# A sequence-mixing kernel's lead reordered: first grams, key spreads, loads and weight pieces

## The chip, the cores and the metric

The kernel runs on one core of one Trainium2 chip. The metric is the time of one execution on the device in microseconds. The four compute engines are TensorE (PE), VectorE (DVE), ScalarE (ACT) and GpSimd (POOL); SyncE (SP) issues all transfers. Each engine takes its own instructions in order and waits on semaphores.

## The reference

Four layers follow each other on a hidden state of 4 sequences x 1024 tokens x 128 channels, each ending in a layer norm over its residual sum:

```
x = layernorm(x + delta_attention(x))   # q, k, v: projection, causal conv of 4 taps, silu
x = layernorm(x + moe(x))               # 8 experts, top 2, 128 -> 256 -> 128, gelu
x = layernorm(x + lru(x))               # gated linear recurrence over tokens
x = layernorm(x + ffn(x))               # gated 128 -> 512, two 512 x 512 gelu layers, 512 -> 128
```

The delta attention has 4 heads of 32 and chunks of 32 tokens. q and k are normalised; per chunk the product of keys with keys (the gram), scaled by beta, is a strictly lower triangular 32x32 matrix A, and T = inverse of (I + A) is needed before the chunk's state step. The state runs through the chunks in order:

```
attn = tril(q_i @ k_i.T);  u_new = u_i - w_i @ S     # u = T v beta, w = T k beta
o_i  = q_i @ S + attn @ u_new;  S = S + k_i.T @ u_new
```

## The kernel before

Tokens are cut into 8 tiles of 128 tokens of all 4 sequences (512 columns, 16 chunks). Most operands are held as two parts (high and low) so that one product is three matmuls. The convolution is folded into the projection: `project(t, m)` is 12 matmuls of 512 columns (4 taps x 3), for m = k, q, v.

For each tile the attention front is: `beta`, `project`, `heads_in` (ACT: silu and square), `squares` (PE: sums per head), `norms_ln` and `norms_exp` (ACT), `unit_rows` (DVE: normalised keys and queries, and turned keys), `key_spread(t, g)` (ACT: keys laid out by head, two halves of 8 chunks), `gram(t, g)` (PE, two halves), `gram_rows(t, g)` (DVE). For every pair of tiles `solve_in` (DVE) turns the grams so that POOL can solve all 128 triangles at once, in 31 rows of two operations (`solve`); `solve_out` (DVE) turns the result back and scales it. The rows are then stored (`store_pack`, `store_tt`) and come back tile by tile. The delta chain of a tile has four steps of `delta_wu` (PE), `delta_spread` (DVE), `delta_attn` (PE), `delta_qp` (DVE), `delta_state` (PE), `delta_out` (DVE); the spread of T by heads is `t_spread` on POOL.

The order of the work is written out by hand, one list for each engine. The lead does the front of tiles 0 to 4 (`LEAD = 5`, lines 368, 499, 860 and 1382). `ramp1(0, 5)` runs the delta chain of tile 0 beside the front of tile 5, `ramp2(0, 6)` the end of tile 0's attention beside the front of tile 6, `dense(0, 1)` the experts of tile 0 (loop over e = 0 to 7) beside the delta chain of tile 1, `ramp3(0, 1, 7)` the recurrence of tile 0, the attention end of tile 1 and the front of tile 7. From then on `dense` and `tails` alternate; the steady ones are not touched.

Weights come from memory in 19 pieces of 512 columns through two buffers (piece p uses buffer p mod 2); `split_pieces` on DVE cuts each into parts. Pieces 0 to 3 and 8 are also centred (four operations more, piece 8 one more for its scaling). In which stage a piece is split is in the table `PIECES`, by stage number. Piece p is loaded (`load_piece`) once piece p - 2 has been split. Buffer 1 lies over the scratch tile m4 of the recurrence. The raw tile `xs` has one buffer: `load_xs(t)` waits for `beta(t-1)` and `split_x(t-1)`, and `split_x(t)` on DVE cuts it into one of two slots. SP's lists are at lines 363 to 403: in the lead, each turn issues `load_xs(t + 2)`, then pieces, then `store_pack(t)`.

In the lead PE does for each tile: squares of t, beta and all three projections of t + 1, then gram(t). DVE ends the lead with `solve_out(0)`; the first `solve` on POOL (line 1148) stands before `ramp1`, whose `t_spread(0, 0)` needs `solve_out(0)`. `ramp1` on PE starts with `project(5, 0)` and `beta(5)`.

## Time and profile before

| | |
|---|---|
| median of 3 runs | 907.69 us (902.43 to 908.14) |
| the profiled execution, its span | 902.85 us, 900.7 us |
| TensorE busy | 815.4 us, 91% of the span |
| VectorE, ScalarE, GpSimd busy | 618.7, 490.2, 480.7 us (69, 54, 53%) |
| mean granted TensorE clock | 0.949 of full speed |
| chain that ended last | PE 57%, DVE 15%, POOL 10%, issue 10%, ACT 5%, DMA 2% |

The rows of a timeline are: start us, length us, engine, line and operation, tile written <- tiles read, shape, count, and in brackets how long the engine had been idle before and what ended that. Line 429 is the helper through which every matmul goes and line 1340 the second half of splitting a piece, so the tile names tell the work. A matmul row's length runs over the start of the next, since matmuls are pipelined. The busy share of PE is not PE at its peak. The lead lasts to about 105 us, ramp1 to 141, ramp2 to 170, dense(0) to 222, ramp3 to 265.

### The profile page before, as it was taken

To read this page: it belongs to the slowest core of one execution; us is meant where nothing else is said; L and a number is where in the kernel's file an instruction comes from. 1 tells how busy PE (TensorE), PEld (TensorE's weight loads), DVE (VectorE), ACT (ScalarE), POOL (GpSimd) and SP (SyncE) were. 2 spreads that over 40 slices of the span, in tenths; PEclk is the share of its full clock that TensorE was granted. 3 is DMA by queue.
4 is the path that set the end of the run, shared out by engine and by line. 5 is a ranking of instruction groups with operands and counts; after the bars stand their busy time and mean duration, and the time that the engine had idled before them with its cause. 6 is when DMAs were issued, how large, how long until landed. Compare 5 with 4: busy or idle time off the path is not lost.

```text
span 900.7 us, 11912 instructions
## 1 busy us (share of the span) xinstructions
PE 815.4 (91%) x3810; PEld 628.3 (70%) x3810; DVE 618.7 (69%) x1166; ACT 490.2 (54%) x768; POOL 480.7 (53%) x508
## 2 busy tenths in 40 slices
PE   5998798897778999999998999999999999999896
PEld 3786685676457777777776778768867886676674
DVE  2777776787759758676867677767677766676352
ACT  2887145334653474357435744575476447667553
POOL 0049697676716637863785355534544453366343
PEclk9999699599969999899999999999999999999998
DMA  3134606301220020002000300200020000000000
GB/s 128 48 99 113 187 1 176 118 12 30 53 59 25 24 59 1 1 25 70 1 1 10 109 1 1 70 24 0 0 70 24 0 0 12 1 0 13 1 12 12
DMA packets 37759, 35.81 MB, mean 40 GB/s; under 512 B 1616, under 2 KB 30544, under 8 KB 37712
## 3 DMA queue, kind: packets, MB, share of 16 engines
q1 hardware_dynamic: 37712, 35.22, 14.0%
q8 instruction: 25, 0.41, 0.2%
q14 instruction: 22, 0.18, 0.1%
HBM read 21.85 MB, written 13.37 MB: 39 GB/s over the span
## 4 chain that ended last, share of the span: by engine, by line
PE 57%; DVE 15%; POOL 10%; issue 10%; ACT 5%; DMA 2%; POOLq 0%; DVEq 0%; ACTq 0%; SPq 0%
PE bank L429 57%; POOL tpm L1133 2%; POOL tmp L1130 2%; POOL fbl L1189 2%; DVE sexp L1428 2%; POOL acc L1197 2%; DVE spread L1412 1%; DVE yg L1438 1%; DMA ws<-in_wf 1%; DVE m L1473 1%; POOL fbl L1220 1%; ACT L1084 1%; POOL fal L1228 1%; DVE fbh L1605 1%; DVE fah L1662 1%
## 5 line engine op out<-in xcount | busy, mean ns | idle before, releaser
L1001 ACT ACTIVATE hf<-bank 128x512 f32<-128x512 f32 x64 | 38.3, 598 | 182.5 <-PE bank L429 176.0
L1189 POOL TENSOR_TENSOR fbl<-hf,fbh 128x512 fp32r<-128x512 f32 x64 | 81.9, 1279 | 81.9 <-DVE fbh L1605 81.9
L1130 POOL TENSOR_TENSOR tmp<-apm,tpm 128x31 f32<-128x31 f32 (+15 forms) x124 | 77.2, 622 | 54.4 <-DVE apm L1302 47.1
L1220 POOL TENSOR_TENSOR fbl<-hf,fbh 128x512 fp32r<-128x512 f32 x32 | 41.3, 1290 | 103.3 <-DVE fbh L1662 103.3
L429 PEld LDWEIGHTS bank<-pk,spread 128*128 128x128 f32 x640 | 82.7, 206 | 18.7 <-DVE spread L1412 11.7
L429 PE MATMUL bank<-pk,spread 128*128 128x64 f32 x640 | 85.2, 291 | 7.4 <-DVE spread L1412 5.6
L1603 DVE TENSOR_TENSOR fbl<-hf,fbh 128x512 fp32r<-128x512 f32 x64 | 59.2, 925 | 34.2 <-ACT fbh L1007 31.7
L1197 POOL TENSOR_TENSOR acc<-acc,yg 128x512 f32<-128x512 f32 x48 | 64.3, 1340 | 33.6 <-DVE yg L1438 33.6
L1133 POOL TENSOR_TENSOR tpm<-tpm,tmp 128x31 f32<-128x31 f32 (+15 forms) x124 | 76.8, 620 | 9.7
L429 PE MATMUL bank<-fal,wfh 128*128 128x512 f32 x160 | 68.3, 427 | 2.7 <-ACT hf L1033 1.6
L1216 POOL TENSOR_TENSOR fal<-hf,fah 128x512 fp32r<-128x512 f32 x32 | 41.6, 1301 | 51.8 <-DVE fah L1657 51.8
L1438 DVE TENSOR_TENSOR yg<-bank,gb 128x512 f32<-128x512 f32 x64 | 43.8, 685 | 35.4 <-PE bank L429 35.3
L429 PE MATMUL bank<-fbl,wmh 128*128 128x512 f32 x128 | 58.8, 460 | 8.4 <-POOL fbl L1189 4.9
L1033 ACT ACTIVATE hf<-bank,vec 128x512 f32<-128x512 f32 x64 | 42.5, 686 | 42.4 <-PE bank L429 42.1
L1228 POOL TENSOR_TENSOR fal<-hf,fah 128x512 fp32r<-128x512 f32 x32 | 41.4, 1298 | 40.6 <-DVE fah L1662 40.6
L429 PE MATMUL bank<-fah,wfh 128*128 128x512 f32 x160 | 62.5, 391 | 0.0
L429 PE MATMUL bank<-fah,wfl 128*128 128x512 f32 x160 | 62.5, 390 | 0.0
L429 PE MATMUL bank<-fbl,wfh 128*128 128x512 f32 x128 | 55.1, 431 | 7.6 <-POOL fbl L1220 7.5
L429 PE MATMUL bank<-x1l,wmh 128*128 128x512 f32 x128 | 55.5, 434 | 0.0
L429 PE MATMUL bank<-x1h,wmh 128*128 128x512 f32 x128 | 52.2, 408 | 0.0
L429 PE MATMUL bank<-x1h,wml 128*128 128x512 f32 x128 | 51.8, 405 | 0.0
L429 PE MATMUL bank<-fbh,wfh 128*128 128x512 f32 x128 | 51.4, 401 | 0.0
(220 smaller groups left out, 2234.9 us busy)
## 6 DMA issues: line engine op xcount, KB each, us to landing
pk<-pack SPq DMA_DIRECT2D x7, 1280.0 KB, 7.1
pack<-pk SPq DMA_DIRECT2D x5, 1280.0 KB, 6.7
ws<-in_wf SPq DMA_DIRECT2D x11, 256.0 KB, 3.5
pack<-pk SPq DMA_DIRECT2D x4, 640.0 KB, 4.4
xs<-in_xh SPq DMA_DIRECT2D x8, 262.0 KB, 4.3
xt<-in_xh SPq DMA_DIRECT2D x8, 262.0 KB, 3.0
ws<-in_wm SPq DMA_DIRECT2D x8, 256.0 KB, 2.7
tt<-ttp SPq DMA_DIRECT2D x4, 512.0 KB, 3.0
```

The lines of the kernel that those rows point to most:

```text
L429: return P.matmul(out, lhsT, rhs, start=start, stop=stop, skip_group_check=skip)
L1001: A.activation(hf[:, 0, :], bank[4][:, :], ACT.Gelu).then_inc(S["gelu_done"], 1)
L1033: A.activation(hf[:, o % 2, :], bank[4 + o][:, :], ACT.Gelu, scale=vec[:, v + o:v + o + 1])\
L1130: G.tensor_tensor(m, a, r, ALU.mult).then_inc(S["t_mul"], 1)
L1133: G.tensor_tensor(o, o, m, ALU.subtract).then_inc(S["t_step"], 1)
L1189: G.tensor_tensor(fbl[:, sl, :], hf[:, 1, :], f32(fbh[:, sh, :]), ALU.subtract)\
L1197: G.tensor_tensor(acc[:, :], (x1 if e == 1 else acc)[:, :], yg[:, (e - 1) % 2, :], ALU.add)\
L1216: G.tensor_tensor(fal[:, c, :], hf[:, c % 2, :], f32(fah[:, c, :]), ALU.subtract)\
L1220: G.tensor_tensor(fbl[:, o, :], hf[:, o % 2, :], f32(fbh[:, o, :]), ALU.subtract)\
L1228: G.tensor_tensor(fal[:, o, :], hf[:, o % 2, :], f32(fah[:, o, :]), ALU.subtract)\
L1438: tt(yg[:, e % 2, :], bank[6][:, :], gb[:, e % 2, :], ALU.mult).then_inc(S["yg_ready"], 1)
L1603: tt(fbl[:, sl, :], hf[:, 0, :], f32(fbh[:, sh, :]), ALU.subtract).then_inc(S["lo0"], 1)
```

## The change

- Lead, PE: after squares(0), beta(1) and projections (1, k) and (1, q) come squares(1), gram(0), beta(2), gram(1), and only then projection (1, v) and those of tile 2. From tile 2 on the order is as before, but the last turn (tile 4) also does beta(5) and projections (5, k) and (5, q) ahead of gram(4).
- The second half of the key spread of tiles 0 and 1 is one DVE operation (`first_spread`, 128x1024) instead of four ACT copies.
- Lead, DVE: solve_in(0) follows gram_rows(1), ahead of the pieces 0 and 1 and value_rows(1). solve_out(0) moves ahead of gram_rows(4), and split_x(6) into the lead.
- SP: load_xs runs further ahead; from the second round on each round is store_pack(t), two pieces, load_xs(t + 3).
- Pieces: `PIECES` is a table by name. Six pieces are split in the lead instead of twelve, two in ramp1 instead of one, two in ramp2 instead of three, six in dense(0) instead of three, three in ramp3 instead of none.
- solve_out(1) and store_tt(1) move from ramp2 into dense(0), split_x(7) from the end of ramp2 into dense(0). The third solve starts in dense(0) (twelve rows there) instead of ramp2 (ten rows there, seven in dense(0)); nineteen rows instead of fourteen are left for ramp3.
- ramp1, PE: starts with projection (5, v); squares(5), projection (6, k) and gram(5) fill the steps. mix_gate stands behind the last step. ACT: beta_in(5) first, heads_in(5, v) last.

```diff
-PIECES = ((0, 1), (2, 3), (4, 5), (6, 7, 8), (9, 10, 11), (12,), (13, 14, 15), (16, 17, 18))
+PIECES = dict(tile1=(0, 1), tile2=(2, 3), tile3=(4, 5), ramp1=(6, 7), ramp2=(8, 9), experts0=(10, 11, 12, 13, 14, 15),
+              ramp3=(16, 17, 18))
 # SP, lead
+            load_pieces(PIECES["tile1"])
             load_x(0)
             load_xs(1)
+            load_xs(2)
+            load_xs(3)
+            store_pack(1)
+            load_pieces(PIECES["tile2"])
+            load_xs(4)
+            store_pack(2)
+            load_pieces(PIECES["tile3"])
+            load_xs(5)
+            store_pack(3)
+            load_pieces(PIECES["ramp1"])
+            load_xs(6)
+            store_pack(4)
             store_tt(0)
 # PE, lead
+            squares(0)
+            beta(1)
+            project(1, 0)
+            project(1, 1)
+            squares(1)
+            gram(0, 0)
+            gram(0, 1)
+            beta(2)
+            gram(1, 0)
+            gram(1, 1)
+            project(1, 2)
+            for m in range(3):
+                project(2, m)
+            for t in range(2, LEAD):
                 squares(t)
+                beta(t + 1)
+                project(t + 1, 0)
+                project(t + 1, 1)
                 if t + 1 < LEAD:
+                    project(t + 1, 2)
                 gram(t, 0)
                 gram(t, 1)
 # DVE, lead
+            def first_spread(t):
+                dve.wait_ge(S["kq_done"], 2 * t + 2)
+                tt(kspread[slot(t)][1], rep(pks[t][:, 8:16, SK:SK + 1, :], 2, NH), heads(8), ALU.mult)\
+                    .then_inc(S["kexp_dve"], 1)
...
+            unit_rows(0)
+            first_spread(0)
+            beta_rows(0)
+            value_rows(0)
+            split_x(2)
+            beta_rows(1)
+            gram_rows(0, 0)
+            gram_rows(0, 1)
+            unit_rows(1)
+            first_spread(1)
+            gram_rows(1, 0)
+            gram_rows(1, 1)
+            solve_in(0)
+            split_pieces(PIECES["tile1"])
+            value_rows(1)
+            split_x(3)
+            for t in range(2, LEAD):
                 unit_rows(t)
                 if t == LEAD - 1:
-                    split_pieces(PIECES[t - 1][2:])
                     solve_in(1)
                 value_rows(t)
+                split_x(t + 2)
                 beta_rows(t)
+                if t == LEAD - 1:
+                    solve_out(0)
+                else:
+                    split_pieces(PIECES[f"tile{t}"])
                 gram_rows(t, 0)
                 gram_rows(t, 1)
 # DVE, dense (m = 0)
-                    if isinstance(m, int) and m == 0 and e in (2, 4, 6):
-                        split_pieces(PIECES[NT - 1][e // 2 - 1:e // 2])
+                    if isinstance(m, int) and m == 0 and e == 1:
+                        solve_out(1)
+                    if isinstance(m, int) and m == 0 and e == 3:
+                        split_x(NT - 1)
+                    if isinstance(m, int) and m == 0 and 2 <= e:
+                        split_pieces(PIECES["experts0"][e - 2:e - 1])
 # DVE, ramps
             def ramp1(a, s):
                 delta_spread(a, 0)
-                split_pieces(PIECES[s])
+                beta_rows(s)
                 delta_qp(a, 0)
                 delta_out(a, 0)
                 delta_spread(a, 1)
+                split_pieces(PIECES["ramp1"][:1])
+                unit_rows(s)
                 delta_qp(a, 1)
-                split_x(s + 1)
...
             def ramp2(a, s):
                 solve_in(2)
-                split_pieces(PIECES[s][:2])
+                split_pieces(PIECES["ramp2"])
                 head_scale(a)
                 unit_rows(s)
                 beta_rows(s)
-                solve_out(1)
...
-                split_pieces(PIECES[s][2:])
-                split_x(s + 1)
             def ramp3(m, a, s):
                 head_scale(a)
                 scale("2", m, m1, m3, x2).then_inc(S["x2"], 1)
+                split_pieces(PIECES["ramp3"][:2])
                 softplus_log()
+                split_pieces(PIECES["ramp3"][2:])
                 lru_input(m)
 # PE, ramp1
-                project(s, 0)
-                beta(s)
+                project(s, 2)
+                pe.wait_ge(S["qkv_act"], 3 * LEAD + 2)
                 delta_wu(a, 0)
-                project(s, 1)
+                squares(s)
                 delta_attn(a, 0)
                 delta_state(a, 0)
                 delta_wu(a, 1)
-                project(s, 2)
+                project(s + 1, 0)
                 delta_attn(a, 1)
                 delta_state(a, 1)
                 delta_wu(a, 2)
-                squares(s)
+                gram(s, 0)
                 delta_attn(a, 2)
                 delta_state(a, 2)
                 delta_wu(a, 3)
-                gram(s, 0)
-                mix_gate(a)
+                gram(s, 1)
                 delta_attn(a, 3)
                 delta_state(a, 3)
-                gram(s, 1)
-                project(s + 1, 0)
+                pe.wait_ge(S["qkv_act"], 3 * LEAD + 3)
+                mix_gate(a)
                 beta(s + 1)
                 project(s + 1, 1)
 # ACT, recurrence of tile 0
+                    act.wait_ge(S["ws_lo"], PIECES["ramp3"][1] + 1)
 # POOL, dense (m = 0)
-                    if isinstance(m, int) and m == 0 and e < E - 1:
-                        solve(2, range(10 + e, 11 + e))
+                    if isinstance(m, int) and m == 0 and e == 1:
+                        solve_init(2)
+                    if isinstance(m, int) and m == 0 and 0 < e < E - 1:
+                        solve(2, range(2 * e - 2, 2 * e))
```

## Rows read from the trace of the kernel before

**Rows 1.** Windows: busy us (instructions) of each engine, granted clock, DMA share, GB/s.
```profile
80.00:100.00 20.00, 16.01 (x74) 13.38 (x73) 17.70 (x28) 8.79 (x16) 17.61 (x29) 0.74 0.42 114
100.00:120.00 20.00, 14.51 (x71) 12.11 (x71) 9.81 (x15) 2.60 (x5) 13.20 (x24) 0.83 0.42 124
```
**Rows 2.** Timeline of PE in the lead and at the start of ramp1.
```profile
24.00 1.98 PE L429 MATMUL bank<-hf,cst 128*128 128x512 f32 x4 [0.38 <-DVE s3row L1379]
...
26.28 0.80 PE L429 MATMUL bank<-xtl,wtaph 128*128 128x512 f32 x1
...
35.17 1.89 PE L429 MATMUL bank<-pk,gb 128*128 128x64 f32 x16
...
88.48 3.38 PE L429 MATMUL bank<-pk,gb 128*128 128x64 f32 x16 [3.87 <-DVE pk L1264]
...
106.58 1.97 PE L429 MATMUL bank<-pk,texp 128*128 128x64 f32 x8 [5.38 <-POOL texp L1159]
```
**Rows 3.** Timeline of POOL: the first solve row, and the spread after it.
```profile
56.41 0.24 POOL L1130 TENSOR_TENSOR tmp<-apm,tpm 128x31 f32<-128x31 f32 x1 [47.06 <-DVE apm L1302]
...
105.28 2.47 POOL L1159 TENSOR_TENSOR texp<-ttp,cst 128x512 f32<-128x512 f32 x2 [5.48 <-DVE ttp L1313]
```
**Rows 4.** Timeline of DVE in the lead.
```profile
62.40 0.43 DVE L1253 CAST xth<-xs 128x524 fp32r<-128x524 f32 x1 [3.23 <-DMA xs<-in_xh]
...
76.62 0.48 DVE L1253 CAST xth<-xs 128x524 fp32r<-128x524 f32 x1 [2.06 <-DMA xs<-in_xh]
...
78.88 0.87 DVE L1338 CAST wmh<-ws 128x512 fp32r<-128x512 f32 x1
...
82.59 0.41 DVE L1291 TENSOR_TENSOR pk<-bank,cst 128x256 f32<-128x256 f32 x1
...
88.22 1.10 DVE L1332 TENSOR_TENSOR ws<-ws,s3row 128x512 f32<-128x512 f32 x1
...
92.71 1.94 DVE L1302 STREAM_TRANSPOSE apm<-kkp 128x1024 f32<-128x1024 f32 x1
...
101.98 1.90 DVE L1311 STREAM_TRANSPOSE ttp<-tpm 128x1024 f32<-128x1024 f32 x1
```
**Rows 5.** Timeline of DVE in ramp1 and ramp2.
```profile
135.66 1.29 DVE L1428 STREAM_TRANSPOSE sexp<-bank 32x128 f32<-32x128 f32 x4 [0.53 <-PE bank L429]
...
149.01 0.43 DVE L1338 CAST wfh<-ws 128x512 fp32r<-128x512 f32 x1 [5.94 <-DMA ws<-in_wf]
...
151.25 0.75 DVE L1455 SCALAR_TENSOR_TENSOR a<-a,vec,a 128x512 f32<-128x512 f32 x1
...
158.18 0.68 DVE L1406 TENSOR_TENSOR x<-bank,a 128x512 f32<-128x512 f32 x1
```
**Rows 6.** Timeline of PE in ramp2 and at the start of dense(0).
```profile
152.05 1.13 PE L429 MATMUL bank<-xt,centre_w 128*128 128x512 f32 x2 [2.66 <-DVE a L1455]
...
173.76 3.68 PE L429 MATMUL bank<-pk,spread 128*128 128x64 f32 x16 [0.90 <-DVE spread L1412]
```
**Rows 7.** Timeline of ACT: the first half of the key spread of tile 0.
```profile
28.38 1.71 ACT L855 ACTIVATE gb<-pk,cst 128x256 f32<-128x256 f32 x4 [0.24 <-DVE pk L1264]
```
**Rows 8.** Timeline of SP, its transfers' issues: a pack store and the next tile's load.
```profile
54.40 0.40 SPq L347 DMA_DIRECT2D pack<-pk  x1
...
56.19 1.07 SPq L326 DMA_DIRECT2D xs<-in_xh  x1
```
**Rows 9.** The page's transfers: KB each, median us from issue to landing.
```profile
xs<-in_xh SPq DMA_DIRECT2D x8, 262.0 KB, 4.3
```
**Rows 10.** Timeline of DVE in dense(0) (two rows) and ramp3 (two rows).
```profile
179.98 0.69 DVE L1603 TENSOR_TENSOR fbl<-hf,fbh 128x512 fp32r<-128x512 f32 x1 [2.37 <-ACT fbh L1007]
...
204.09 0.79 DVE L1603 TENSOR_TENSOR fbl<-hf,fbh 128x512 fp32r<-128x512 f32 x1 [1.12 <-ACT fbh L1007]
...
238.05 0.72 DVE L1463 TENSOR_SCALAR m<-m 128x512 f32<-128x512 f32 x1 [0.71 <-ACT m L918]
...
240.07 0.69 DVE L1406 TENSOR_TENSOR x<-bank,a 128x512 f32<-128x512 f32 x1 [1.30 <-ACT a L883]
```

More of the change, by code:

```diff
@@ L859, in _ @@
             act.wait_ge(S["w_in"], 32)
-            for t in range(LEAD):
+            for m in range(3):
+                heads_in(0, m)
+            beta_in(0)
+            A.preload_act_table_set(LN_EXP)
+            norms_ln(0)
+            norms_exp(0)
+            act.wait_ge(S["sp_step"], 1)
+            A.activation(spv[:, 1:2], spv[:, 0:1], ACT.Exp, scale=-1.0).then_inc(S["sp_step"], 1)
+            A.preload_act_table_set(SILU)
+            heads_in(1, 0)
+            key_spread(0, 0)
+            heads_in(1, 1)
+            beta_in(1)
+            A.preload_act_table_set(LN_EXP)
+            norms_ln(1)
+            norms_exp(1)
+            key_spread(1, 0)
+            A.preload_act_table_set(SILU)
+            heads_in(1, 2)
+            for t in range(2, LEAD):
                 for m in range(3):
@@ L1180, in ramp3 @@
                 t_spread(a + 1, 1)
-                solve(2, range(17, C - 1))
+                solve(2, range(12, C - 1))
             def dense(m, a, f, inv=0):
```

81 lines of the change are left out of this document (30 added, 51 removed).

## The prediction

> **What bounds the kernel now.** I read the windows of the first 120 us first: in 80 to 120 us, where the lead gives way to the first ramp, TensorE has gaps and its granted clock falls to 0.74 and 0.83 of 2.4 GHz [rows 1]. Nothing behind the third ramp is changed, so only the time up to there can move.
>
> The PE timeline names the two gaps [rows 2]. The gram of tile 4 stands 3.87 us behind that tile's normalised keys, since no lead product is left to fill; and the first delta product, at 106.58, stands 5.38 us behind a spread on POOL. After a gap products run at half speed: a gram half that took 1.89 at 35.17 takes 3.38 at 88.48. POOL's first triangular solve starts at 56.41, once the grams of tiles 0 and 1 are through DVE, and ends 5.48 us before 105.28, at 99.80: 43.4 us [rows 3]. DVE turns the result at 101.98 and hands it on 3.2 us later [rows 4]. So the delta chain waits for solve, DVE and POOL in series.
>
> From there to the dense stage DVE sets the end: it stands 5.94 us before a weight piece until 149.01, comes to head_scale at 151.25 [rows 5], and PE waits 2.66 us for it [rows 6].
>
> **The change part by part.**
>
> *Lead: PE and solve.* The squares of tile 0 start at 24.0 as before. From 26.7 to 35.17 run three projections, 2.83 us each; squares take 1.8, a beta 0.86, a gram half 1.75 (1.89 less its drain) [rows 2]. After beta(1) and two projections PE is at 32.4; squares(1) waits for the second activation of tile 1, which stands on ACT behind a table load, an activation pair and key_spread(0,0), four copies in 1.71 us [rows 7]: about 34.8. Both halves of gram(0) end at 38.4, beta(2) at 39.3. DVE takes gram_rows(0) ahead of unit_rows(1), so tile 1's keys come at 40.0, ACT's copies end at 41.75 and gram(1,0) starts at 41.9: a new PE gap of 2.6 us. DVE's key spread (1024 columns) has no row; its bounds are nothing, where it lies wholly beside ACT's copies, and 1.9, as the 1024-column transpose at 101.98 [rows 4]; I take 1.2, and hide it behind those copies and the first gram half, which together last 3.4. gram(1) ends at 45.4, solve_in(0) at 48.3; POOL starts 8 us earlier and ends at 91.7.
>
> PE is then 3.4 us behind the old order with the same work done, so the squares of tile 4 end at 87.8. But the old gap of 3.87 now holds two projections of tile 5.
>
> *Lead: DVE and loads. Here I think the gain is lost.* solve_out(0) stands on DVE behind split_x(6) and beta_rows(4), and split_x(6) needs load_xs(6). SP now goes pack store, two pieces, load_xs, each round. In the old order pack(1) is issued at 54.40, xs(4) at 56.19, and DVE waits 3.23 us for it until 62.40 [rows 4, 8]: 8.0 us from the issue of the store, where the median of such loads is 4.3 [rows 9]. So a load waits for the 1.28 MB ahead of it. The two pieces (0.51 MB) between them add from nothing to 2.7 us (in proportion to 1.54 MB in 8.0 us); I take 1.5, near the middle, so 9.5. Then, with a centred piece at 4.5 less 1.1 for its scaling, 3.35 (88.22 to 92.71), a plain one at 1.86 (two in 78.88 to 82.59), split_x with beta_rows at 2.3 (76.62 to 78.88) and gram_rows at 1.4:
> store_pack(1) needs value_rows(1), behind two centred pieces: 48.3 + 6.7 + 0.7 = 55.7; xs(4) lands at 65.2. store_pack(2) at 65.2 + 2.3 + 6.7 + 1.4 = 75.6; xs(5) at 85.1. store_pack(3) at 85.1 + 2.3 + 3.7 + 1.4 = 92.5; xs(6) at 102.0. Then 2.3, solve_out 3.2, the spread 1.3 and 0.3 of handing on: the first delta product at 109.1, not 106.58: **+2.5**. With the pieces at nothing it is -2, with 2.7 each it is +6. PE has ended project(5,2) near 102 and idles seven us, so half speed follows as before.
>
> The Trainium skill (DMA: Bandwidth & Descriptors, Queues, rings and completion order) says that a completion's semaphore write lands only after every earlier write of that DMA engine; by that rule a load can't be seen before the store ahead of it, and the term would lie above, not below, +2.5.
>
> *Ramp 1.* Before, 29.1 us run from the first delta product to the end of the last state product at 135.66 [rows 2, 5]. Each step is a chain: spread, attention, qp, state, transposes. Step 0 exchanges a projection for the shorter squares (-0.9); step 1 gets piece 6 and unit_rows ahead of qp on DVE (+2.3 beyond its old filler); steps 2 and 3 lose split_x and unit_rows (-1.1). Sum **+0.3**. PE's two projections fewer give nothing: the chain bounds.
>
> *Ramp 2.* DVE's 5.94 wait and two pieces in 2.24, together 8.2, give way to value_rows 0.7, piece 8 with its scaling 4.5 and piece 9 1.86: **-1.1**. PE now waits over 4 us for head_scale, as long as the gap ahead of 88.48, so I charge half speed for its next two products and the variance: **+0.9**. solve_out(1), which leaves its place ahead of the normalisation at 158.18, lay beside ACT's chain; its exposure is between 0 and 3.2, I take **-0.7**, the time of one ACT operation. The piece and split_x that leave the end of the ramp put DVE ahead of the first expert spread, but PE waited only 0.90 for that [rows 6]: **-0.9**. Together with the lead, the dense stage starts at +1.0.
>
> *Dense(0).* DVE gets solve_out(1) at e=1, split_x at e=3 and pieces at e=3, 5, 7, beside those that stood at e=2, 4, 6. A plain piece takes 1.12 alone (149.01 to 151.25) and 1.86 beside POOL, which works here. The idle that stood at these places [rows 10] is 2.37 at e=1, and 1.12 at e=5, and the same once more at e=7. Exposed: 3.2 - 2.4 = 0.8 at e=1, 1.3 + 1.9 at e=3, 0.7 at e=5 and 0.7 at e=7: **+5.4**. POOL gets twelve short rows and two memsets for seven long rows; I charge nothing, covered by its waits for DVE; that cover is the third rival's point.
>
> *Ramp 3.* Three pieces stand around the softplus steps, two before POOL is busy: 1.12 + 1.12 + 1.86 = 4.1, less the idle of 0.71 and 1.30 behind them [rows 10]: **+2.1**. ACT's decay now waits for piece 17 as well, which is done before softplus is. POOL's five more rows, seven us, end in its idle before the next stage.
>
> Sum +1.0 + 5.4 + 2.1 = **+8.5 us**. The profiled execution took 902.85 (span 900.7), 4.8 under the median of 907.69; four executions lie two at 902.4 to 902.9 and two at 907.7 to 908.1. Against the profile the sum is 911.4, against the median 916.2; not knowing the level of the next runs I count from the middle, 905.3: 913.8.
>
> **The rivals.** *The loads are not held* (16%). xs lands 4.3 us after its issue, DVE never waits, solve_out(0) ends at 99.2, the first delta product is at 100.5: -6.1; with -1.0 for full clock in step 0 and +0.3 - 1.1 + 0.9 - 0.7 - 0.9 as above the dense stage starts at -8.6; +5.4 + 2.1 leave -1.1: 904.2. For it: the median of 4.3. Against: 62.40.
>
> *All of it arrives* (16%). As above, and the added DVE work falls into DVE's idle of dense(0) and ramp 3, while the pack store freed from pieces ahead of it gives up to 2.4 more at the start of dense(0): -11, 894.3. Against: the idle stands at other places than the additions.
>
> *DVE and POOL collide in dense(0)* (25%). The place is e=1 to 7, with twelve solve rows on POOL and six pieces on DVE. A piece cost 1.86 instead of 1.12 where they met. If it costs 2.4, and POOL's doubled rows use up the idle of e=5 and 7, the stage pays 0.8 + 3.7 + 2.4 + 2.4 = 9.3 and ramp 3 3 x 2.4 - 2.0 = 5.2: +15.5 with the start's 1.0, 920.8. It decides from pieces over 2.0 us on average. The Trainium skill (SBUF — State Buffer, Who interferes with whom) speaks for this one: a VectorE operation with two SBUF inputs and a reading GpSimd operation exclude each other for whole instructions. By that rule, the trace agrees as far as the 1.86 goes.
>
> **How the numbers follow.** Forecast 43% (from -1 to +13 by its bounds, 904 to 918), rivals 16, 16 and 25. One per cent, 9.1 us, is what a measurement can tell. Slower by more: the third rival's 25 and 9 of the forecast's, 0.34. Faster by more: 0.16. The rest, 0.50. The range, 897 to 922, leaves out most of the second rival and the end of the third.
>
> **What would show it.** DVE's xs casts of tiles 5 and 6 near 85 and 102 behind a DMA (without a wait: first rival); POOL's first solve row near 48; a PE gap of 2.6 near 39; the first delta product near 109; DVE idle gone at e=3 of dense(0) and pieces there over 2.0 (third rival); ramp 3 two us longer. The forecast is wrong if the first delta product comes before 104, or if dense(0) takes no longer than before.

## The result, and the profile of the changed kernel

The changed kernel takes 917.05 us in the median of four runs (914.88 to 918.04), the kernel before 906.03 beside it (902.43 to 908.14): a ratio of 1.0123, 95% interval 1.0081 to 1.0165. It is slower. The middle of the interval lies a little beyond the one per cent that I called the limit of a measurement, and its lower end lies within it. The profiled execution took 914.88 us with a span of 912.9, against 902.85 and 900.7: 12.2 us more in the span, where I had summed 8.5.

The ledger of the two profiled executions, by landmarks that both have. The last columns are for the experiments below.

| landmark (start, us) | before | changed | xs first | piece later | lead | best | relief |
|---|---|---|---|---|---|---|---|
| first delta product | 106.58 | 111.11 | 103.80 | 110.79 | 102.85 | 102.72 | 104.19 |
| last state transposes of ramp1 | 135.66 | 145.40 | 138.89 | 134.13 | 126.69 | 126.15 | 128.00 |
| head_scale of ramp2 | 151.25 | 157.21 | 150.84 | 147.96 | 140.40 | 135.26 | 137.03 |
| attention norm of ramp2 | 158.18 | 163.56 | 157.18 | 155.82 | 148.51 | 144.64 | 146.41 |
| first attention product of dense(0) | 173.76 | 177.00 | 171.18 | 170.18 | 162.71 | 160.95 | 162.37 |
| sum at the end of dense(0) | 221.35 | 227.98 | 222.18 | 221.74 | 215.80 | 211.48 | 210.82 |
| attention norm of ramp3 | 240.07 | 250.31 | 244.51 | 243.89 | 238.10 | 230.38 | 229.66 |
| first spread of dense(1) | 265.95 | 277.88 | 272.08 | 271.82 | 266.01 | 258.72 | 258.61 |
| span | 900.7 | 912.9 | 907.2 | 907.5 | 901.6 | 894.2 | 897.8 |

Between the first two columns: +4.5 at the first delta product, +5.2 in ramp1, -6.5 from there to the dense stage, +3.4 in dense(0), +5.3 in ramp3, and 0.3 in all that follows. Predicted were +2.5, +0.3, -1.8, +5.4 and +2.1.

The last row of the table needs care. Behind the first spread of dense(1) the orders of all kernels here are the same, but eleven of the fourteen profiled executions take 634.8 to 636.0 us from there to the end, and three take 638.8 to 639.5: the projection as filler, the early softplus and relief. So some 4 us of a span can come from a part that no edit touches, and versions are best compared by the rows above.

The windows of the changed kernel, with busy us and instructions of each engine, granted clock, DMA share and GB/s. The first two answer to [rows 1]:

```profile
80.00:100.00 20.00, 20.00 (x113) 16.34 (x111) 11.68 (x20) 15.86 (x29) 11.28 (x22) 1.00 0.62 169
100.00:120.00 20.00, 14.81 (x73) 12.10 (x73) 12.04 (x22) 6.53 (x10) 10.27 (x20) 0.74 0.44 135
120.00:140.00 20.00, 18.25 (x99) 18.01 (x98) 11.26 (x23) 5.18 (x10) 18.16 (x26) 0.63 0.05 13
```

The last window in the kernel before:

```profile
120.00:140.00 20.00, 18.91 (x136) 16.31 (x135) 17.20 (x36) 11.02 (x18) 18.20 (x26) 1.00 0.00 1
```

In 80 to 100 us the change has done what its order says: TensorE has no gap and the upper level of its clock (1.00, against 0.74). But in 120 to 140 us, where the kernel before ran at 1.00, the granted clock is 0.63. The lower level is where ramp1 loses its time.

TensorE's timeline, beside [rows 2] and [rows 6]:

```profile
41.30 1.97 PE L433 MATMUL bank<-pk,spread 128*128 128x64 f32 x16 [2.31 <-issue]
...
105.85 0.77 PE L433 MATMUL bank<-xtl,wtaph 128*128 128x512 f32 x1 [5.18 <-ACT yg L855]
...
111.11 1.25 PE L433 MATMUL bank<-pk,texp 128*128 128x64 f32 x8
...
124.03 1.10 PE L433 MATMUL bank<-qpc,sexp 128*128 128x64 f32 x8 [1.75 <-DVE qpc L1479]
...
126.38 3.62 PE L433 MATMUL bank<-pk,gb 128*128 128x64 f32 x16
...
158.01 1.13 PE L433 MATMUL bank<-xt,centre_w 128*128 128x512 f32 x2 [0.70 <-DVE a L1514]
...
199.02 2.47 PE L433 MATMUL bank<-pk,spread 128*128 128x64 f32 x16 [3.18 <-DVE spread L1471]
```

POOL's, beside [rows 3], and its sum of experts in dense(0):

```profile
49.38 0.24 POOL L1171 TENSOR_TENSOR tmp<-apm,tpm 128x31 f32<-128x31 f32 x1 [39.96 <-DVE apm L1343]
...
108.52 2.50 POOL L1200 TENSOR_TENSOR texp<-ttp,cst 128x512 f32<-128x512 f32 x2 [15.59 <-DVE ttp L1354]
...
191.66 1.75 POOL L1236 TENSOR_TENSOR acc<-acc,yg 128x512 f32<-128x512 f32 x1
```

ScalarE's, the last beta of the lead:

```profile
105.11 0.60 ACT L855 ACTIVATE yg<-bank 128x512 f32<-128x512 f32 x1 [6.04 <-DVE yg L1319]
```

DVE's in the lead, beside [rows 4]:

```profile
88.21 0.43 DVE L1294 CAST xth<-xs 128x524 fp32r<-128x524 f32 x1 [6.38 <-DMA xs<-in_xh]
...
103.23 0.43 DVE L1294 CAST xth<-xs 128x524 fp32r<-128x524 f32 x1 [5.03 <-DMA xs<-in_xh]
...
104.32 0.70 DVE L1319 STREAM_TRANSPOSE yg<-yg 128x512 f32<-128x512 f32 x1
...
105.14 1.98 DVE L1352 STREAM_TRANSPOSE ttp<-tpm 128x1024 f32<-128x1024 f32 x1
```

SP's issues, beside [rows 8]:

```profile
79.18 0.39 SPq L350 DMA_DIRECT2D pack<-pk  x1
79.63 3.16 SPq L336 DMA_DIRECT2D ws<-in_wm  x2
82.89 1.24 SPq L329 DMA_DIRECT2D xs<-in_xh  x1
93.98 0.40 SPq L350 DMA_DIRECT2D pack<-pk  x1
...
97.59 1.22 SPq L329 DMA_DIRECT2D xs<-in_xh  x1
```

DVE's in the ramps and in dense(0), beside [rows 5] and [rows 10]:

```profile
120.14 0.89 DVE L1381 TENSOR_TENSOR wml<-ws,wmh 128x512 fp32r<-128x512 f32 x1
...
123.71 0.27 DVE L1479 TENSOR_TENSOR qpc<-cst,bank 128x128 f32<-128x128 f32 x1
...
152.75 0.65 DVE L1373 TENSOR_TENSOR ws<-ws,s3row 128x512 f32<-128x512 f32 x1
...
157.21 0.74 DVE L1514 SCALAR_TENSOR_TENSOR a<-a,vec,a 128x512 f32<-128x512 f32 x1
...
186.50 1.64 DVE L1381 TENSOR_TENSOR wfl<-ws,wfh 128x512 fp32r<-128x512 f32 x1
...
190.60 1.66 DVE L1296 TENSOR_TENSOR xtl<-xs,xth 128x524 fp32r<-128x524 f32 x1
192.19 1.51 DVE L1379 CAST wfh<-ws 128x512 fp32r<-128x512 f32 x1
...
237.71 1.66 DVE L1381 TENSOR_TENSOR wfl<-ws,wfh 128x512 fp32r<-128x512 f32 x1
...
246.93 0.55 DVE L1379 CAST wfh<-ws 128x512 fp32r<-128x512 f32 x1
...
250.31 0.68 DVE L1465 TENSOR_TENSOR x<-bank,a 128x512 f32<-128x512 f32 x1
```

The first two rows are the last operation of piece 6 and the last of the qpc pair in step 1 of ramp1. Between them stands unit_rows, and it is 3.8 us from the start of the one to the end of the other; TensorE waits 1.75 us of that. From 152.75 to 157.21 are both pieces of ramp2, at 190.60 and 192.19 the split and a piece of expert 3, and at 237.71 and 246.93 pieces of ramp3.

POOL's first solve row comes 7.0 us sooner and the solve ends 15.6 us before POOL's next work, but nothing is gained: its result is turned at 105.14 only, behind split_x(6), which waited 5.03 us for its load. That is the read of the whole lead: what is ready at 92.9 stands in a queue behind something that isn't.

### The profile page after: what moved, and what is told of

Its sections match the earlier page's. It is cut to its first block, busy times and chain, and to the rows that moved or that the text cites. A ratio compares the mean times of both kernels' runs of the same rounds, so it can differ in the third digit from the quotient of the medians.

```text
span 912.9 us, 11905 instructions
## 1 busy us (share of the span) xinstructions
PE 826.6 (91%) x3810; PEld 637.9 (70%) x3810; DVE 623.9 (68%) x1168; ACT 485.6 (53%) x759; POOL 481.6 (53%) x508
## 4 chain that ended last, share of the span: by engine, by line
PE 60%; DVE 19%; ACT 7%; issue 6%; POOL 6%; DMA 1%; SPq 0%; DVEq 0%; POOLq 0%; ACTq 0%
PE bank L433 60%; DVE sexp L1487 2%; DVE yg L1497 1%; DVE spread L1471 1%; DVE m L1532 1%; POOL fbl L1228 1%; POOL acc L1236 1%; DVE fbl L1665 1%; POOL tpm L1174 1%; POOL fbl L1261 1%; POOL tmp L1171 1%; DVE fbh L1667 1%; ACT L1125 1%; DVE x L1465 1%; POOL fal L1269 1%
## 5 line engine op out<-in xcount | busy, mean ns | idle before, releaser
L433 PEld LDWEIGHTS bank<-pk,spread 128*128 128x128 f32 x640 | 84.7, 211 | 21.9 <-DVE spread L1471 11.1
L433 PE MATMUL bank<-pk,spread 128*128 128x64 f32 x640 | 87.4, 296 | 11.5 <-DVE spread L1471 6.8
L433 PE MATMUL bank<-fbh,wml 128*128 128x512 f32 x128 | 51.9, 406 | 0.0
L433 PE MATMUL bank<-fbh,wmh 128*128 128x512 f32 x128 | 51.8, 405 | 0.0
```

The lines of the kernel that those rows point to most:

```text
L433: return P.matmul(out, lhsT, rhs, start=start, stop=stop, skip_group_check=skip)
```

## Experiments

Each is the changed kernel with the edit shown. The kernel before ran beside them, with medians from 903.8 to 904.7.

### The loads ahead of the stores

```
-            store_pack(2)
-            load_pieces(PIECES["tile3"])
             load_xs(5)
-            store_pack(3)
-            load_pieces(PIECES["ramp1"])
+            store_pack(2)
+            load_pieces(PIECES["tile3"])
             load_xs(6)
+            store_pack(3)
+            load_pieces(PIECES["ramp1"])
             store_pack(4)
```

> The changed kernel, with SP issuing load_xs(5) and load_xs(6) ahead of the pack store and the two pieces of their round, nothing else moved. Theory (a load waits behind the store and the pieces issued before it): DVE's casts of xs for tiles 5 and 6, which stood at 88.2 behind 6.4 us and at 103.2 behind 5.0 us of waiting, come near 82 and 98 with almost no wait; with them ACT's activation of beta of tile 5 and PE's last v projection, which waited 5.2 us, move from 105.9 to about 100; the first delta product comes near 104 to 105 instead of 111.1. The whole is 5 to 8 us faster than the changed kernel. Rival (the loads are late by themselves, or DVE is busy anyway): the casts stay within 1.5 us of 88 and 103, and the whole within 2 us.

It took 908.98 us (ratio to before 1.0031, interval 1.0002 to 1.0060). The casts of tiles 5 and 6 start at 81.69 and 96.88 and wait for nothing; project(5, 2) starts at 100.89 and the first delta product at 103.80, 7.3 us sooner than with the change. But ramp1 then takes 35.1 us, and this is its window:

```profile
120.00:140.00 20.00, 20.00 (x91) 19.42 (x91) 8.29 (x20) 0.00 (x0) 17.96 (x28) 0.50 0.05 14
```

Twenty us at the lower level throughout. Of the head start of 7.3 us, 5.7 reach the end of the span, and the loss in ramp1 is a separate one.

### A projection as filler in step 2 of ramp1

```
                 delta_wu(a, 2)
+                project(s + 1, 1)
                 gram(s, 0)
...
                 beta(s + 1)
-                project(s + 1, 1)
```

> The changed kernel with the k-side projection's neighbour, projection (6, q), moved on PE from the end of ramp1 into step 2, ahead of the first gram half of tile 5. No work is added. Theory (in ramp1 the clock fell to half from 125 to 149 us and the steps of 64-column products kept it there, while 512-column projections held it in the kernel before): with a projection in step 2 the clock is back at full speed by step 3, step 3 takes about 7 us instead of 10.5, and ramp1's end comes 2 to 5 us earlier. Rival (the delta chain through DVE bounds each step, the clock only fills idle time): the projection lengthens step 2 by its 2.9 to 5 us and the end comes no earlier, or up to 3 us later.

913.16 us (1.0082, 1.0048 to 1.0116). The gap ahead of step 1's product from qpc is there as before (1.72 us at 122.73), the two products behind it run at the lower level, and then the projection brings the upper level back: the window 120 to 140 has 0.83, and the last step takes 6.0 us instead of 10.2. Step 2 pays for the projection (10.4), so the last transposes come at 141.16, 4.2 us sooner, of which 1.0 was there already at the first delta product (110.11).

### Piece 6 one step later

```
                 delta_spread(a, 1)
-                split_pieces(PIECES["ramp1"][:1])
                 unit_rows(s)
                 delta_qp(a, 1)
                 delta_out(a, 1)
                 delta_spread(a, 2)
+                split_pieces(PIECES["ramp1"][:1])
                 delta_qp(a, 2)
```

> The changed kernel with the split of piece 6 on DVE moved from step 1 of ramp1 (ahead of unit_rows of tile 5) to step 2. Theory (the PE gap of 1.75 us at 122.3 us, made by piece 6 and unit_rows ahead of qp1, is what drops the clock): the gap shrinks to under 0.5 us, the clock stays at full speed in step 2, and the last transposes of ramp1 come 4 to 6 us earlier than 145.4. Rival (the low column count of the steps themselves drops it, gap or not): the clock falls within a few us all the same, and only the 1.4 us of the piece are gained.

910.45 us (1.0066, 1.0033 to 1.0100). The window:

```profile
120.00:140.00 20.00, 18.75 (x137) 16.53 (x137) 16.54 (x37) 8.21 (x17) 18.22 (x25) 1.00 0.10 27
```

The products of steps 1 and 2 on TensorE's timeline:

```profile
121.55 1.09 PE L433 MATMUL bank<-qpc,sexp 128*128 128x64 f32 x8
...
123.36 1.95 PE L433 MATMUL bank<-pk,gb 128*128 128x64 f32 x16
...
125.47 2.00 PE L433 MATMUL bank<-pk,spread 128*128 128x64 f32 x16 [0.16 <-DVE spread L1471]
```

There is no wait before the product from qpc at 121.55, where the changed kernel has 1.75 us, and the gram half behind it takes 1.95 us at the upper level. From the first delta product to the last transposes the ramp takes 23.3 us against 34.3: 1.5 us of DVE's work at the wrong place cost 11. By steps, 1.9 of the 11 are step 1, with the wait in it, and 8.8 are steps 2 and 3 at the lower level (10.0 and 10.2 us against 5.7 and 5.7). The steps' products are the same in both runs, so their small size alone didn't lower the clock: the rival falls. This is the largest single thing that the runs found. Of the 11.3 us won there, 6.8 are left at the first attention product of dense(0): now DVE's chain of solve_in(2) and both pieces is what head_scale waits for, beside POOL's second solve, which had ended before in the slow ramp.

### The third solve and solve_out(1) back in ramp2

```
-                solve(2, range(12, C - 1))      # POOL, ramp3
+                solve(2, range(17, C - 1))
...
+                solve_init(2)                   # POOL, ramp2
+                solve(2, range(10))
...
                 beta_rows(s)                    # DVE, ramp2
+                solve_out(1)
                 attention_norm(a)
```

In dense(0) one row stands at each of experts 0 to 6 again, and solve_out(1) leaves expert 1.

> The changed kernel with one part undone: solve_out(1) is back in ramp2, and POOL's third solve starts in ramp2 with ten rows, seven in dense(0) and fourteen in ramp3, as before the change. Pieces and split_x stay where the change put them. Theory (what dense(0) and ramp3 cost is DVE's own queue of pieces): dense(0) gets shorter by 1 us or less, ramp3 by at most 1, the whole is within 2 us. Rival (POOL's doubled rows beside DVE's pieces make the cost, by collisions): dense(0) gets shorter by 3 us or more and ramp3 by 2, the whole is 4 us faster.

915.27 us (1.0126, 1.0079 to 1.0173): no gain in total. Dense(0) is not shorter (51.9 us from its first attention product, against 51.0), so neither the short rows nor solve_out(1) were what lengthened it. But ramp3, from the sum to the first spread, takes 46.1 us instead of 49.9; the kernel before took 44.6. Nine profiled executions with nineteen rows left for ramp3 and no edit in it take 49.8 to 50.4 us there, so five solve rows more or less on POOL are 3.8 of ramp3's 5.3 us. What is gained so is paid before it: the dense stage starts 1.9 us later, with solve_out(1) in ramp2, and takes 0.9 more.

### The lead: three edits together

The loads first, `beta_rows(4)` ahead of `split_x(6)` on DVE, and piece 6 one step later.

> Three edits to the lead and first ramp together: the xs loads of tiles 5 and 6 are issued ahead of the pack stores, the last lead tile's beta rows stand ahead of the split of tile 6 on DVE, and piece 6 stands in step 2 of the first ramp. Theory (the lead's two waits and one late DVE wait that costs TensorE its clock): the first delta product comes near 103.8, the ramp runs at the upper level in 23.5 us, its last state transposes stand near 127.5 against 145.40 with the change, the dense stage starts 12 or more us earlier, and of that 9 to 12 us reach the end: 903 to 906. Rival (what is won ahead of the ramp is given back to the loads of the second ramp, which wait for its first pack store): the end comes at 909 to 912 as with each edit alone.

902.02 us, ratio to before 0.9968 (0.9945 to 0.9990): a little better than I expected, and faster than both kernels (than the kernel before by 0.3 per cent). The two losses add up: the first delta product at 102.85, ramp1 in 23.8 us, the dense stage 14.3 us sooner than with the change. By the first spread of dense(1) 11.9 of them are left; 2.1 were lost in dense(0), 0.3 in ramp3.

### Beta rows alone

```
-                split_x(t + 2)
-                beta_rows(t)
+                if t == LEAD - 1:
+                    beta_rows(t)
+                split_x(t + 2)
+                if t < LEAD - 1:
+                    beta_rows(t)
```

> The changed kernel with one edit: in the last lead round beta_rows(4) stands on DVE ahead of split_x(6), which waits 5.03 us for its load, instead of behind it. Theory (the missed step: beta_in(5) on ACT waits for these rows, and project(5,2) for beta_in(5)): project(5,2) starts near 92 to 98 instead of at 105.85, and is done before the solve is turned; but the first delta product still waits for solve_out(0), behind the same load, so it comes at 109.5 to 110.5 instead of 111.11, and the total stays within 2 us of 917. Rival (the projection at half speed is what holds the first delta product): it comes at 107 or earlier, and the total falls by 4.

918.34 us (1.0165, 1.0122 to 1.0208). Project(5, 2) starts at 100.45, later than I expected but done before the turn, and the first delta product comes at 108.94, 2.2 us sooner, but now behind a gap, and at the lower level. TensorE's timeline:

```profile
108.94 1.94 PE L433 MATMUL bank<-pk,texp 128*128 128x64 f32 x8 [5.42 <-issue]
110.68 3.73 PE L433 MATMUL bank<-hf,cst 128*128 128x512 f32 x4
```

Four square products take 3.73 us instead of 1.94, and the last transposes come at 146.30. What the late projection had cost it had given back as a warm clock: alone, the edit is worth nothing.

### Ramp2: head_scale ahead of the pieces

```
                 solve_in(2)
-                split_pieces(PIECES["ramp2"])
                 head_scale(a)
                 unit_rows(s)
                 beta_rows(s)
+                split_pieces(PIECES["ramp2"])
                 attention_norm(a)
```

> As the kernel with three edits to the lead and first ramp, and in the second ramp pieces 8 and 9 stand on DVE behind head_scale, unit_rows and beta_rows instead of ahead of them. Theory (head_scale stands behind 6 us of pieces, and TensorE waits 3.8 us for it and falls to half speed): head_scale comes 5 to 6 us sooner, TensorE's gap ahead of the product from a shrinks below 1 us, the products of the gram and the router in this ramp run at the upper level, and the dense stage starts 4 to 6 us sooner than without this edit. Rival (the ramp is bound by DVE's total work): the pieces are then late for the attention norm and the start of the dense stage moves by under 2 us.

It has the three edits of the lead too: 901.56 us (0.9963, 0.9945 to 0.9982). head_scale comes at 135.54, 4.9 us sooner, and the norm at 148.09, 0.4 us sooner. DVE waits 3.36 us for a transfer ahead of unit_rows and then does both pieces while ScalarE's 1 / deviation has been ready since 143.6. The dense stage starts at 162.27 instead of 162.71. The rival was right: the pieces were late for the norm instead.

### Dense(0): the split of tile 7 at expert 6

```
-                    if isinstance(m, int) and m == 0 and e == 3:
+                    if isinstance(m, int) and m == 0 and e == 6:
                         split_x(NT - 1)
```

> The changed kernel with one edit: the split of tile 7's input stands at expert 6 of dense(0) on DVE instead of expert 3. Theory (the 2.1 us of split ahead of fbl, the transposes and the spread of expert 3 are what TensorE waits for): its wait of 3.18 us for the third delta spread of dense(0) falls to about 1.1, and dense(0) takes 1.5 to 2.5 us less than its 50.98, the total 915. Rival (DVE's total work bounds dense(0)): the wait turns up at expert 6 and 7, dense(0) takes what it took, 917.

918.37 us (1.0147, 1.0105 to 1.0190). TensorE's wait for the third spread falls from 3.18 to 1.89, and another of 2.86 appears ahead of the down product at 224.09 (it was 1.37); dense(0) takes 52.1 us. The rival held: moving work within the stage moves the wait.

### Dense(0): six subtractions made twice

```
+                    if p in PIECES["experts0"]:
+                        tt(low_of(p), buf_of(p)[:, :], f32(high_of(p)), ALU.subtract).then_inc(S["sub_once"], 1)
+                        dve.wait_ge(S["sub_once"], p - PIECES["experts0"][0] + 1)
                     tt(low_of(p), buf_of(p)[:, :], f32(high_of(p)), ALU.subtract).then_inc(S["ws_lo"], 1)
```

> The changed kernel with the subtraction of pieces 10 to 15 made twice, the second behind the first; what is computed is the same. Six more two-input operations of DVE in dense(0), 0.93 to 1.65 us each by the trace, 8 to 9 us of DVE's time. Theory (DVE's queue bounds dense(0), and each us of piece there is a us of the stage but for the two idle places behind the spreads): dense(0) grows from 50.98 by 5 to 8 us, so the price of a piece there is about 70 to 100 per cent of its time, and the six pieces and one split explain the whole difference to the kernel before. Rival (TensorE's own work and gates bound it, and pieces fall into the wait for yg): it grows by under 3 us.

920.97 us (1.0188, 1.0149 to 1.0228). The second subtractions take 0.69, 0.75, 0.79, 0.86, 0.97 and 0.96 us, 5.0 together where I had expected 8 to 9, and dense(0) takes 56.6 us instead of 51.0, 5.6 more: each us of DVE's time at the places of the pieces is a us of the stage, with nothing hidden. At expert 1 it isn't so: with solve_out(1), 3.2 us, taken out there (and POOL's rows put back) the stage took 51.9. TensorE's waits in the stage:

```profile
186.72 2.00 PE L433 MATMUL bank<-pk,spread 128*128 128x64 f32 x16 [0.64 <-DVE spread L1474]
...
201.17 3.67 PE L433 MATMUL bank<-pk,spread 128*128 128x64 f32 x16 [4.62 <-DVE spread L1474]
...
217.78 2.13 PE L433 MATMUL bank<-pk,spread 128*128 128x64 f32 x16 [2.07 <-DVE spread L1474]
```

The wait for the third spread grows from 3.18 to 4.62 and for the fourth from 1.24 to 2.07.

### The softplus steps in the lead

```
             value_rows(1)
             split_x(3)
+            softplus_log()
...
                 split_pieces(PIECES["ramp3"][:2])
-                softplus_log()
                 split_pieces(PIECES["ramp3"][2:])
```

> The changed kernel with one edit: the 21 small steps of the softplus stand in the lead on DVE, behind the split of tile 3 where DVE waits for tile 2's keys, instead of in the third ramp. Theory (in the third ramp DVE's chain of pieces and small steps is what the attention norm waits for, 7.6 us of it the steps): the norm of the third ramp comes 4 to 7 us after head_scale less than the 16.5 us it takes now, until ACT's decay or the variance of the attention is the bound, and the total falls by 4 to 6 us to 911 to 913. Rival (the variance product and ACT bound the ramp, DVE's chain runs beside): the norm stays at 16 us behind head_scale and the total at 917.

918.28 us (1.0138, 1.0099 to 1.0176). The norm of ramp3 follows head_scale after 14.0 us, between the 16.5 of the change and the 9.5 to 12.5 that I expected. The steps had covered a load, as the timelines of DVE and SP show:

```profile
241.15 1.67 DVE L1381 TENSOR_TENSOR wfl<-ws,wfh 128x512 fp32r<-128x512 f32 x1
248.84 0.43 DVE L1379 CAST wfh<-ws 128x512 fp32r<-128x512 f32 x1 [6.01 <-DMA ws<-in_wf]
```

```profile
245.38 0.33 SPq L307 DMA_DIRECT2D xt<-in_xh  x1
245.75 0.43 SPq L336 DMA_DIRECT2D ws<-in_wf  x1
```

Piece 16 has left the buffer of piece 18 at 240.77, but SP issues the load of piece 18 only at 245.75, behind the next tile's xt in its own queue. DVE now waits 6.01 us for it, in the place where the steps had stood for 7.6. In the lead they take 7.6 us too, and the first delta product comes 2.1 us later.

### A version made of what the runs point to

The three edits of the lead; in ramp2 head_scale, piece 8, unit_rows, beta_rows, the norm, piece 9; the softplus steps in the lead; piece 18 behind the first gram rows of ramp3.

> A version made of what the runs point to: xs loads of tiles 5 and 6 ahead of the stores, beta rows ahead of the split, piece 6 in step 2 of the first ramp, in the second ramp head_scale ahead of piece 8 and the norm ahead of piece 9, the softplus steps in the lead in DVE's idle ahead of tile 2's keys (7.0 us with the loads so ordered), piece 18 behind the first gram rows of the third ramp. Theory: the dense stage starts 3 to 4 us sooner than with the lead edits and pieces behind head_scale alone (the norm at 144 to 145), and the third ramp takes 5 to 7 us less from head_scale to the norm: 891 to 896. Rival (DVE stays late in the lead because the steps don't fit the idle, and POOL's solve rows slow the third ramp as before): 898 to 902.

901.15 us in the median of twelve (895.96 to 902.43), ratio 0.9953 (0.9932 to 0.9974). The profiled execution, at 895.96, is the lowest of them; eight lie at 900 to 902.4, so the median is in the rival's band and the profile in mine. The norm of ramp2 comes at 144.64 as expected, but the dense stage starts only 1.3 us sooner than with the pieces behind head_scale (160.95 against 162.27), where I had expected 3 to 4. In ramp3 the norm follows head_scale after 13.1 us, 3.4 less than with the change; I had expected 5 to 7. DVE's timeline of ramp3 shows three waits, all for ScalarE now:

```profile
219.61 1.52 DVE L1379 CAST wfh<-ws 128x512 fp32r<-128x512 f32 x1
221.17 1.65 DVE L1381 TENSOR_TENSOR wfl<-ws,wfh 128x512 fp32r<-128x512 f32 x1
224.95 1.08 DVE L1524 SCALAR_TENSOR_TENSOR m<-m,x 128x512 f32<-128x512 f32 x1 [2.13 <-ACT m L948]
228.37 0.71 DVE L1526 TENSOR_SCALAR m<-m 128x512 f32<-128x512 f32 x1 [2.33 <-ACT m L957]
230.38 0.69 DVE L1469 TENSOR_TENSOR x<-bank,a 128x512 f32<-128x512 f32 x1 [1.31 <-ACT a L921]
```

### The same with expert 3 of dense(0) relieved

```
-                    if isinstance(m, int) and m == 0 and e == 3:
-                        split_x(NT - 1)
-                    if isinstance(m, int) and m == 0 and 2 <= e:
-                        split_pieces(PIECES["experts0"][e - 2:e - 1])
+                    if isinstance(m, int) and m == 0 and e in (2, 4, 5, 6, 7):
+                        j = max(e - 3, 0)
+                        split_pieces(PIECES["experts0"][j:j + 1])
...
             def ramp3(m, a, s):
+                split_x(NT - 1)
+                split_pieces(PIECES["ramp3"][:2])
                 head_scale(a)
                 scale("2", m, m1, m3, x2).then_inc(S["x2"], 1)
-                split_pieces(PIECES["ramp3"][:2])
+                split_pieces(PIECES["ramp3"][2:3])
```

The table gives five pieces to dense(0) and four to ramp3; SP loads piece 17 ahead of the next tile.

> As the version made of what the runs point to, and one more edit: nothing is added at expert 3 of dense(0) on DVE. Its piece and the split of tile 7 leave the stage; in their place split_x(7) and pieces 15 and 16 stand at the start of the third ramp ahead of head_scale, where DVE idles 5.12 us and POOL waits for a load; piece 17 follows head_scale. Theory (DVE's queue bounds dense(0): two subtractions of it doubled there cost their full time): TensorE's wait of 3.18 us for the third spread falls to about 1, dense(0) takes 3 to 5 us less than the 49.2 it takes in that version, the third ramp stays within 1 us of its 47.2, and the total is 3 to 4 us below 901. Rival (TensorE's and POOL's chain through the experts is right behind DVE's): dense(0) falls by under 1.5 us.

898.10 us (894.04 to 900.64, six runs), ratio 0.9922 (0.9894 to 0.9950), the lowest median of all; but its interval and that of the version without this edit overlap, and the two profiled executions stand level at the first spread of dense(1), 258.61 against 258.72. That the edit shortens the whole is not shown. Dense(0) takes 48.5 us from its first attention product against 50.5 (the 49.2 in the expectation was my misreading). That is 2.1 us, between theory and rival: the wait for the third spread falls from 3.18 to 0.96, and the one for the fourth grows from 1.24 to 2.48.

```profile
182.96 2.00 PE L434 MATMUL bank<-pk,spread 128*128 128x64 f32 x16 [0.96 <-DVE spread L1476]
...
196.10 2.00 PE L434 MATMUL bank<-pk,spread 128*128 128x64 f32 x16 [2.48 <-DVE spread L1476]
```

DVE's timeline at the start of ramp3:

```profile
212.95 0.69 DVE L1382 TENSOR_TENSOR wfl<-ws,wfh 128x512 fp32r<-128x512 f32 x1
...
214.01 0.69 DVE L1382 TENSOR_TENSOR wfl<-ws,wfh 128x512 fp32r<-128x512 f32 x1
216.34 0.75 DVE L1519 SCALAR_TENSOR_TENSOR a<-a,vec,a 128x512 f32<-128x512 f32 x1 [1.64 <-ACT a L939]
```

Two pieces cost 1.1 us each there, with POOL idle, and head_scale still waits 1.64 us for ScalarE.

## Why the prediction came out as it did

**The time lies in the range**, 3.3 us over the forecast of 913.8, and in part that is luck. The third rival's 920.8 is hardly further off, so the time alone doesn't choose between them; the stages do. Within one per cent was the likeliest class, with 0.50, and the result is 1.2 per cent slower, for which I had 0.34; its interval, 0.8 to 1.65 per cent, doesn't exclude the first. The sum was better than its terms: the lead, ramp1 and ramp3 were taken too small by 2.0, 4.9 and 3.2 us, ramp2 and dense(0) too large by 4.7 and 2.0: errors of 10.1 us one way and 6.7 the other, and that they cancel so far is the luck in it.

**The lead: DVE did wait for the loads, for another reason than I gave, and one wait was missed.** The solve row came at 49.38 (forecast 48), TensorE's gap with 2.31 us at 41.30 (2.6 near 39), the casts with waits of 6.38 and 5.03 us at 88.21 and 103.23 (85 and 102). From the issue of the store to the cast behind the load it is 9.03 and 9.25 us; I had taken 9.5, from the 8.0 that stood there without the pieces.

But "a load waits for the 1.28 MB ahead of it" is the smaller part of this time. SP issues the loads only 3.71 and 3.61 us behind the store (79.18 to 82.89, 93.98 to 97.59), since its two piece issues take 3.16 us in the first case and 3.07 in the second, and the casts start 5.32 and 5.64 us behind the loads' own issue, where the median landing of such a load is 4.1 us in this kernel's trace. In the kernel before, the 8.0 us were 1.79 to the issue and 6.21 behind it. In the changed kernel SP also stands at the store first, until DVE's rows for it are there, with the load behind it in its list. With the loads first, the load of tile 6 is issued at 91.94, ahead of the store at 92.44, and neither cast waits. The stores themselves came at 79.18 and 93.98 where my working had 75.6 and 92.5. So SP's order is shown to be the cause, and how much of the 1.2 and 1.5 us over the median the store's bytes cost is not. The first rival (not held) was near in the landing and wrong in saying that DVE never waits: 4.3 us behind 82.89 is 87.2, still 5.4 us after DVE was free.

The Trainium skill (DMA: Bandwidth & Descriptors, Queues, rings and completion order) has a completion seen only after every earlier write of its DMA engine; these runs fit with that, but don't separate it from plain sharing of bandwidth.

What failed is the sentence that TensorE has ended project(5, 2) near 102. It has to wait for bank 3, so for ScalarE's beta_in(5), so for DVE's beta_rows(4), which stands behind the same split_x(6): 105.85, at half speed, to 111.1. With it the term was +4.5, not +2.5. In the run with beta rows alone that projection is out of the way, and the first delta product comes at 108.94, where 109.1 had been forecast; 0.8 us of that run's gain is beta_rows(4) itself, which no longer stands behind the load. I had followed the new wait to solve_out(0) and not to the other things queued behind it.

**Ramp1: the step that failed.** "Sum +0.3 ... the chain bounds." What DVE adds to step 1 was sized well: the step took 8.4 us (116.80 to 125.17) against 6.8 before, 1.6 more, and I had added 2.3 for it. But the wait that this makes on TensorE, 1.75 us, was not followed to the clock. I had charged half speed behind the longer gaps, and none here. The products of steps 2 and 3 then ran at the lower level (a gram half in about 3.6 us instead of 1.95), and with the wait itself this was 11 us with piece 6 at step 1 and nothing with piece 6 at step 2. The other half of the sentence failed too, the other way. Without the wait the ramp takes 23.3 us, 5.8 less than the 29.1 before, so the two projections that left it did give something; most of it is step 0, 5.7 us in the changed kernel against 9.4 before, where I had taken 0.9 off. There the projection had run mostly at half speed behind the gap of 5.38 us (12 products from 108.31 to 113.17, 4.9 us), and I had priced it at full speed.

**Ramp2: right in kind, too small.** -6.5 instead of -1.8. Both pieces took 4.5 us, not 6.4: POOL's second solve ended at 153.8, since ramp1 was so long, and the pieces ran almost alone. With piece 6 one step later the solve still ran beside them, and they took 6.0. TensorE's gap ahead of head_scale's product was 0.70 us where I had feared four, so the charge for half speed was wrong, and the lower level that the kernel before shows from 160 to 180 us (0.51) was in part escaped (0.81 and 0.68 in the same two tens of us); from the norm to the dense stage it is 13.4 us against 15.6.

**Dense(0): +3.4, forecast +5.4.** The bound was named rightly: DVE's queue, worst at expert 3. The doubled subtractions show a price of a full us per us once the idle is gone. The change itself paid less, since the stage had more idle to give than the 4.6 us at three places that I subtracted: DVE was idle for 11.0 of the 47.6 us before and for 4.3 of the 51.0 with the change, so of 10.0 us more work 6.6 went into idle. The third rival, pieces over 2.0 us by collision with POOL, is half true. Five of the six pieces take 2.1 to 2.3 us there (about 0.6 and 1.64) and one 1.6, on average 2.1, so the sign that I had named for it was there, and my 1.86 was too low. But the three pieces there in the kernel before took 2.1, 2.3 and 1.6 too, and with the solve rows put back the stage doesn't get shorter. The subtraction takes 0.69 us alone and 1.64 beside a POOL operation, and even the cast took 1.51 instead of 0.42 at 192.19, beside POOL's sum of experts, which ends at 193.4. The Trainium skill (SBUF — State Buffer, Who interferes with whom) says that either operation blocks the other for its whole length; the trace agrees, since 1.51 is about the rest of POOL's operation (1.2) and then the cast (0.42).

**Ramp3: +5.3, forecast +2.1.** The pieces were sized at 4.1 us and took 5.8, as the second met POOL's spreads (3.2 us instead of 1.1). That collision costs nothing to be seen: in the run with the split at expert 6 both pieces take 1.1 us and ramp3 still takes 50.2. "POOL's five more rows, seven us, end in its idle" was the failed step: with the rows back in place 3.8 us of the stage are gone, and of its 5.3 only 1.5 are left for the three pieces. Which of DVE's operations beside those rows carry the 3.8 is not shown; that they are the long ones of the recurrence is my reading.

## To carry to other kernels

When a wait is added to an in-order engine, list everything queued behind it, and follow each item to its own waiter; here two of three led to the same product, and only one was found. SP is such an engine too: a load comes as late as its place in SP's list makes it, whatever the transfer takes. A short wait on TensorE has two prices, its length and the clock of what follows: in a chain of small products a filler of DVE of 1.5 us ahead of the step's own operation cost 11. Small steps that look like waste may be the cover of a load; before moving them, see what comes due behind them.

## What the runs showed of the hardware

- After one wait of 1.75 us the granted clock was 0.51 for 24 us, through the small products of steps 1 to 3 (125 to 149 us). The same wait, of 1.49 to 1.79 us, stands in seven of the other runs. In the six of them without the moved projection step 2 took 10.1 to 10.2 us, against 5.7 where the wait is gone (piece later, lead). With the projection moved among them the window 120 to 140 has 0.83 against 0.63, and without the wait it has 1.00.
- Behind the gap of 5.18 us project(5, 2) ran at half speed and ramp1 then began at full speed. With that projection ahead of the gap (5.42 us), the first delta product and the squares ran at half speed instead: a filler behind a gap pays for the clock of what follows.
- Even VectorE operations on one column grow beside GpSimd's: in the softplus steps of ramp3 those with two inputs took 0.34 to 0.59 us in the changed kernel, where the first two took 0.21 and 0.16, while nearly all of those with one input stayed at 0.14 to 0.15.
- SyncE's issues are not free: one piece or tile is issued in 0.33 us where nothing is ahead of it, but in the changed kernel's lead the two pieces behind a pack store took 3.05 to 3.16 us, and the load right behind them 1.24 and 1.22.
